# Turning the attended heads by 32x32 block transposes on VectorE instead of transposes on PE, with VectorE's order in an iteration laid out anew

## The reference, cut to what matters

```
x = x + tanh(g_ffn[0])   * L0_ffn(layernorm(x))
x = x + tanh(g_xattn[1]) * L1_xattn(layernorm(x), ctx, ctx, mask)
x = x + tanh(g_ffn[1])   * L1_ffn(layernorm(x))

# L1_xattn: 16 heads of 16 channels, 256 queries, 256 keys
scores = q_h @ k_h.T / 4                       # per head
attn   = softmax(scores)                       # over the keys
out_h  = attn @ v_h                            # 256 x 16 per head
out    = concat(out_h) @ w_o.T + b_o
```

## Time and profile before

| | us |
|---|---|
| median of 3 runs | 1606.79 |
| lowest and highest of the 3 | 1606.21, 1613.41 |
| the profiled execution | 1611.25 |
| its span, first to last instruction | 1609.4 |

### The profile page before, as it was taken

How to read it: one execution, slowest core, us unless ns; L and a number is a source line. 1 busy time by engine, 2 the same in 40 slices (tenths; PEclk the granted TensorE clock), 3 DMA queues, 4 the chain that set the end, 5 groups by cost and what they waited for, 6 DMA issues and landing times.

```text
span 1609.4 us, 42630 instructions
## 1 busy us (share of the span) xinstructions
PE 1483.6 (92%) x14155; PEld 1141.0 (71%) x14155; DVE 1318.3 (82%) x3187; ACT 1135.4 (71%) x2057; POOL 1030.6 (64%) x1392
## 2 busy tenths in 40 slices
PE   3899999999999974478999999999999999999997
PEld 2788888888888863245676677777777777767666
DVE  4798888888888876787888889898988888898732
ACT  7798888888888743265666666676666666666664
POOL 4688888888888743324456565666656565665445
PEclk8899999999999995588999999999999999999999
DMA  6322322322322002422222232233322332233100
GB/s 225 107 73 67 96 67 65 97 65 74 89 65 72 1 1 85 139 83 72 78 81 75 83 88 79 79 87 85 87 81 78 84 86 78 82 83 86 56 17 21
DMA packets 197690, 125.45 MB, mean 78 GB/s; under 512 B 44400, under 2 KB 196848, under 8 KB 197360
## 3 DMA queue, kind: packets, MB, share of 16 engines
q1 hardware_dynamic: 197616, 124.48, 26.7%
HBM read 92.69 MB, written 25.17 MB: 73 GB/s over the span
## 4 chain that ended last, share of the span: by engine, by line
PE 46%; SPq 6%; DMA 3%; DVE 2%; issue 2%; POOL 1%; ACT 1%; POOLq 0%
PE b_bank L1837 27%; PE b_bank L1912 6%; PE b_scoreT L1894 4%; PE b_score L1877 4%; PE b_bank L1845 2%; SPq L1293 2%; DMA b_nmT<-b_nm 1%; SPq L1282 1%; PE b_bank L1989 1%; SPq L1309 1%; PE b_bank L1927 1%; DMA b_yT<-b_y 1%; SPq L1318 1%; DVE b_nm L1653 1%; SPq L1326 1%
## 5 line engine op out<-in xcount | busy, mean ns | idle before, releaser
L1471 ACT ACTIVATE b_E<-b_scoreT 128x1024 f32<-128x1024 f32 x256 | 262.2, 1024 | 151.4 <-PE b_scoreT L1894 151.1
L1653 DVE TENSOR_REDUCE b_nm<-b_score 128x4 bf16<-128x1024 f32 x256 | 313.3, 1224 | 57.4 <-PE b_score L1877 51.2
L31 ACT ACT_TABLE_LOAD x157 | 201.4, 1283 | 18.6 <-PEq L1059 15.2
L1837 PE MATMUL b_bank<-f,b_YT 128*128 128x256 bf16 x1536 | 193.0, 277 | 4.7 <-POOL b_YT L1404 4.6
L890 PE MATMUL bank<-hT,W1T 128*128 128x256 bf16 x1536 | 183.3, 273 | 2.4 <-DVE hT L706 1.6
L1837 PE MATMUL b_bank<-b_hT,f 128*128 128x256 bf16 x1536 | 183.4, 273 | 0.8 <-DVE X L1749 0.8
L890 PE MATMUL bank<-W2T,G 128*128 128x256 bf16 x1024 | 171.0, 272 | 6.7 <-DVE GT L780 6.2
L1837 PEld LDWEIGHTS b_bank<-f,b_YT 128*128 128x128 bf16 x1536 | 144.7, 99 | 40.8 <-issue 19.3
L1837 PEld LDWEIGHTS b_bank<-b_hT,f 128*128 128x128 bf16 x1536 | 147.7, 98 | 30.4 <-issue 12.6
L890 PEld LDWEIGHTS bank<-hT,W1T 128*128 128x128 bf16 x1536 | 147.9, 98 | 27.8 <-ACT G L549 4.1
L1388 POOL TENSOR_TENSOR b_v<-b_v,b_e 128x512 f32<-128x512 f32 x32 | 40.7, 1270 | 194.1 <-DVE b_e L1734 194.1
(11 more groups left out here) (222 smaller groups left out, 3537.1 us busy)
## 6 DMA issues: line engine op xcount, KB each, us to landing
b_Q<-q_dram SPq DMA_DIRECT2D x192, 64.0 KB, 2.5
b_K<-k_dram SPq DMA_DIRECT2D x192, 64.0 KB, 2.7
xin<-in_x SPq DMA_DIRECT2D x32, 256.0 KB, 3.1
ctxn<-in_ctx SPq DMA_DIRECT2D x32, 256.0 KB, 2.8
mask_in<-in_mask SPq DMA_DIRECT2D x32, 256.0 KB, 3.0
X<-in_x SPq DMA_DIRECT2D x32, 256.0 KB, 4.0
ctxt<-in_ctxT SPq DMA_DIRECT2D x32, 256.0 KB, 4.2
b_ctxt<-in_ctxT SPq DMA_DIRECT2D x32, 256.0 KB, 2.8
```

Of the source, the lines that this page charges most:

```text
L31: act.add_instruction(mybir.InstLoadActFuncSet(name=nc.get_next_instruction_name(), act_func_set_id=which, ins=[], outs=[]))
L1471: nc.scalar.activation(E[:, pair:pair + 2], scoreT_ps[:, :, :, :], ACT.Exp).then_inc(sig["E"], 1)
L1653: nc.vector.tensor_reduce(pair, score_ps[:, :, :, :], AX.X, ALU.max, negate=True).then_inc(sig["nm"], 1)
L1837: last = nc.tensor.matmul(out_tile, lhs(i, k), rhs(j, k), start=start and k == chunks[0] and (i, j) == TERMS[0], stop=stop and k == chunks ...
```

## The change

VectorE turns the heads itself. heads_turned(c) is a transpose of each 32x32 block, straight from the PSUM bank to at; since one head's 32 rows fill one block of partitions, this puts tokens on partitions, 32 at a time. inverse_sums and attended divide in SBUF, and heads_back turns the blocks again into oF, channels down the partitions. ScalarE's heads_copy and PE's three groups of four transposes are gone. attended_high now reads oF, and attended_low moves from VectorE to GpSimd, behind rounded. The new steps for c = 0 all stand in the iteration of the values (stage a); those for c = 1 follow in the next one, but for heads_turned(1). Banks 8 and 9 lose the turns OT0, ON and OT1; AV01 and AV23 are now freed by heads_turned ("at").

VectorE's list is in another order. scaled, binades, mlp_columns, magic and base all stand between maxima 0 and 1; statistics_3 moves behind maxima 5 and heads_turned(0), statistics_2 behind maxima 6; mlp_normalised moves from the start of the next iteration to behind maxima 7. On GpSimd inverse_std_2 now stands ahead of silu_parts 0. PE's list is the same but for the transposes. On the host the rows of w_o and b_v are permuted to fit. Of the diff, in this order: GpSimd's new step and its list, ScalarE's attended_high, VectorE's new steps, PE's list.

```diff
+                def attended_low():
+                    pool.wait_ge(sig["onhi"], done(o))
+                    fence()
+                    nc.gpsimd.tensor_tensor(oT[:, 1], oF[:, :, :], oT[:, 0], ALU.subtract).then_inc(sig["onlo"], 1)
...
                 if o:
+                    attended_low()
                     inverse_std_3()
-                if h:
-                    silu_parts(h, 0)
                 if f:
                     inverse_std_2()
                 if h:
+                    silu_parts(h, 0)
                     silu_parts(h, 1)
...
                 def attended_high():
-                    act.wait_ge(sig["onT_mm"], done(o))
+                    act.wait_ge(sig["oF"], done(o, per=C))
...
+                def heads_turned(c):
+
+                    dve.wait_ge(sig["av_mm"], done(a, per=NH // HG, part=2 * c + 2))
+                    nc.vector.transpose(at[:, 2 * c:2 * c + 2].rearrange("p g b r -> p (g b r)"),
+                                        flat_bank(BANK[("AV01", "AV23")[c]])).then_inc(sig["at"], 1)
+
+                def inverse_sums(c, b):
+                    dve.wait_ge(sig["at"], done(b, per=C, part=c + 1))
+                    nc.vector.reciprocal(rsum[:, 2 * c:2 * c + 2, :], at[:, 2 * c:2 * c + 2, :, DK]).then_inc(sig["rsum"], 1)
+
+                def attended(c, b):
+                    dve.wait_ge(sig["rsum"], done(b, per=C, part=c + 1))
+                    nc.vector.tensor_tensor(on[:, c].rearrange("p b g d -> p g b d"), at[:, 2 * c:2 * c + 2, :, 0:DK],
+                                            rsum[:, 2 * c:2 * c + 2, :].rearrange("p g (b u) -> p g b u", u=1).to_broadcast(
+                                                [P, 2, Q32, DK]), ALU.mult).then_inc(sig["on"], 1)
+
+                def heads_back(c, b):
+
+                    dve.wait_ge(sig["on"], done(b, per=C, part=c + 1))
+                    if (due := done(b, back=1)) is not None:
+                        dve.wait_ge(sig["onlo"], due)
+                    nc.vector.transpose(oF[:, c, :], on[:, c].rearrange("p b g d -> p (b g d)")).then_inc(sig["oF"], 1)
...
-                if o:
-                    heads_transposed(0)
                 if m:
                     scores(0)
-                if o:
-                    heads_transposed(1)
...
-                if o:
-                    attended_transposed()
```

More of the change, by code:

```diff
@@ L1501, in attended_high @@
                 def attended_high():
-                    act.wait_ge(sig["onT_mm"], done(o))
+                    act.wait_ge(sig["oF"], done(o, per=C))
                     if (due := done(o, back=1)) is not None:
                         act.wait_ge(sig["proj_mm"], due)
[L1505 to L1512, removed]
+                    nc.scalar.activation(oT[:, 0], oF[:, :, :], ACT.Copy).then_inc(sig["onhi"], 1)
                 def values_copy():
@@ L1556, in iteration @@
                     exponential(6)
-                    heads_copy(0)
                     exponential(7)
@@ L1629, in mlp_normalised @@
                 def mlp_normalised():
[L1630 to L1631 removed]
+                    dve.wait_ge(sig["rs3"], done(o))
+                    if (due := done(o, back=1)) is not None:
                         dve.wait_ge(sig["hT_mm"], due)
                     for t in range(T):
[L1634 removed]
+                        last = nc.vector.tensor_scalar(hn[:, t, :], Xb(o, t), mv3[:, t, 0:1], rh3[:, t:t + 1], ALU.subtract,
                                                        ALU.mult)
@@ L1693, in keys_low @@
                     last.then_inc(sig["klo"], 1)
[L1695 to L1705, removed]
@@ L1775, in iteration @@
                     last.then_inc(sig["f1lo"], 1)
-                if o:
-                    attended(1)
+                if n:
+                    scaled()
+                    binades()
+                if h:
+                    mlp_columns()
+                if n:
+                    magic()
+                if h:
+                    base()
                 if m:
@@ L1785, in iteration @@
                     queries_low()
-                if o:
-                    attended_low()
                 if m:
                     maxima(3)
-                if h:
-                    mlp_columns()
-                if n:
-                    binades()
                 if at_iteration(half, parity, 1):
@@ L1797, in iteration @@
                     quantised_update()
-                if h:
-                    base()
-                if n:
-                    magic()
                 if m:
@@ L1809, in iteration @@
                     maxima(5)
+                if a:
+                    heads_turned(0)
+                if o:
+                    statistics_3()
+                if m:
                     maxima(6)
+                if f:
+                    statistics_2()
                 if w:
                     result()
-                if f:
-                    statistics_2()
+                if m:
+                    maxima(7)
+                if o:
+                    mlp_normalised()
+                if a:
+                    inverse_sums(0, a)
+                if f:
+                    attention_normalised()
+                if a:
+                    attended(0, a)
+                    heads_turned(1)
+                    heads_back(0, a)
                 if q:
                     mask_bias()
-                if m:
-                    maxima(7)
-                if f:
-                    attention_normalised()
                 if at_iteration(half, parity, 3):
@@ L2100, in col, with by_heads @@
         return np.ascontiguousarray(np.reshape(inputs[name], (-1, P)).T)
+    def by_heads(rows):
+        grid = np.reshape(rows, (2, 2, 4, DK, -1))
+        return np.ascontiguousarray(np.reshape(np.transpose(grid, (0, 2, 1, 3, 4)), (NH * DK, -1)))
     arrays = {
```

47 lines of the change are left out of this document (15 added, 32 removed).

## The result

The changed kernel takes 1859.9 us in the median of 4 runs (1858.3 to 1863.6), against 1607.0 for the kernel before beside it (4 runs, 1606.2 to 1613.4): a ratio of 1.157, 95% interval 1.153 to 1.160. It is slower by 252.9 us. The prediction had 1817 in a range of 1640 to 1890. Of the runs of the kernel before, one of those beside e9_store_between was slow, 1939.8 us at a granted clock of 0.74, and stands in no comparison here.

A forecast was written before the change was run, and what follows sets the result against it. PE was taken to set the pace at 28.2 us an iteration. 11.3 + 21.82 + 2.6 = 35.7 us, plus 0.85 for the clock, times 25 gave 915 against 704.6 us: +210, so 1817 us, range 1640 to 1890.

The forecast's parts named there:

- PE's 1.26 us: Three groups of four transposes leave PE at 0.42 us each: 1.26 us an iteration, at most 31 us in all.
- The 21.82 us: PE's time from scores(2) to the next scores(0), with two removed transpose groups of 0.42 us taken off.
- The transposes: VectorE's new 32x32 transposes: 0.68 us for 512 elements from PSUM, 0.42 us for 256.
- Maxima 0 to 1: VectorE's steps there are held up by GpSimd; maxima(1) ends at 11.25 us, scores(2) start at 11.3, 6.6 late.
- One for one: Between maxima 0 and 1, eight VectorE instructions go at GpSimd's pace, each waiting out the GpSimd instruction then running.
- The means named as a sign: If right, mean times of v, e, X and tg on VectorE rise to 0.7 us and more.
- Maxima 7 to the end: hidden(3) on PE waits for heads_turned(1), with hn and xh held by GpSimd: 2.6 us late.
- The clock: PE's idling lowers its granted clock; half the 1.7 us price of one drop taken, 0.85 us an iteration.
- one such drop is no rule: Reason given for charging only half of the single clock drop seen in the kernel before: 0.85 us.
- Rival 2: The clock pays in full, twice an iteration, for both PE idle stretches: +273 us, 1880 us; chance 0.12.
- (1): VectorE's forms aren't hindered at the new place: 29.8 us an iteration, 1648 us; chance 0.12, a part of it 0.16.
- (3): GpSimd becomes the bound: the projection waits 1.6 us for attended_low; +9 us, 1616 us; chance 0.04.

The follow-up runs named there:

- e9_store_between: e6_both with hn's transposes ahead of xh's, scaled between maxima 3 and 4, and SyncE's store ahead of row_of_maxima: 1602.09 us, ratio 0.9961 to the kernel before.
- e6_both: Changed kernel, five VectorE steps at old places, attended_low ahead of rounded, heads_turned(1) directly behind maxima 7: 1610.18 us, ratio 1.0013 to the kernel before.
- e5_pe_filled: Changed kernel with the query product made four times into the same bank, 36 matmuls more an iteration: 1827.84 us.
- experiments 1: Kernel before, PE's transposes kept, with scaled, binades, mlp_columns, magic and base put between maxima 0 and 1: 1816.99 us.
- e4_pool_narrow: Changed kernel with GpSimd's context_parts, both biases and silu_parts cut to 8 columns of each tile (output not the reference's): 1675.98 us.
- Experiment 3: Changed kernel with heads_turned(1) put directly behind maxima 7, ahead of mlp_normalised: 1777.64 us.
- e2_steps_back: Changed kernel with the five moved VectorE steps back at their old places and attended_low ahead of rounded on GpSimd: 1683.04 us.
- e8_low_last: e2_steps_back, but with attended_low left behind rounded on GpSimd, as the change has it: 1866.17 us.

## Why the prediction was right, and where its sizes were off

**What bounds the kernel.** Right: PE paces the kernel before, and the places between the maxima decide, not the totals. One reading was off, and nothing hangs on it: in the iteration that was read, two gaps of 0.21 are put down to another engine and not one (the second at 1223.89, to ScalarE's b_E).

**PE's 1.26 us.** Right in kind and small: taken off PE, they show up only in e6_both to e9_store_between, in part, as means of 27.7 to 27.9 us an iteration against 28.2. The 21.82 us from scores(2) to the next scores(0), which have 0.84 of them taken off, are borne out: e5_pe_filled needs 24.31 less the 2.46 of hidden(3), or 21.85.

**The transposes.** 0.68 and 0.42 were taken; 0.70 to 0.72 and 0.40 to 0.45 were measured. The Trainium skill (VectorE: DVE Perf Modes, "The three transpose paths") led to an estimate of 1.24 for the larger one, from its bfloat16 figure; the measurement decides, and it is 0.70.

**Maxima 0 to 1.** The mechanism was right and is shown by experiments 1 and 4. Ends behind scores(0), forecast and measured: scaled 4.2 and 4.4, binades 5.6 and 5.8, tg 6.1 and 6.3, up 7.3 and 6.5, magic 8.1 and 7.9, base 10.0 and 9.3, maxima(1) 11.25 and 10.5. "One for one" failed in the middle: up slipped into the gap where tg had just come through, and magic began just ahead of GpSimd's biases, which took 1.70 instead of 1.41; whether magic or base held them isn't shown. Two steps that the prediction ran unhindered were held: on (0.82 for 0.42) and dn (1.12 for 0.15), both with two inputs in SBUF. That the end comes out only 0.77 us too late, 19 us in all, is luck: the errors nearly cancel. The means named as a sign rose to 0.7 and more for X (0.77) and binades (1.34), but v and tg are at 0.58 and magic at 0.41.

The Trainium skill (SBUF — State Buffer, "Who interferes with whom") says that VectorE's two-port forms contend with GpSimd, its forms with two SBUF inputs with a GpSimd instruction that reads SBUF, and that the one that issues first blocks the other. The rows on on, dn and the biases agree, the last in GpSimd's disfavour.

**Maxima 7 to the end.** 2.6 us late was forecast and 2.46 measured, for the reason given: hn 1.92 and xh 1.48 stand ahead of the transpose, at GpSimd's pace. Experiment 3 shows that this order is the cause, and experiment 4 GpSimd's part in it: with GpSimd short, 0.46 of the 2.46 are left.

**The clock.** This is the term that was mis-sized. Half the price of one drop, 0.85 us an iteration, was taken; 27.02 - 21.82 - 2.46 = 2.74 us was measured, and experiment 5 gives 2.7 by another way. That is 1.89 us an iteration more than was taken, 47 us over 25 iterations. The step that failed is "one such drop is no rule": it was one, with a drop in every iteration. Rival 2 had the size better (3.4 us an iteration) but the wrong form: it priced two drops of 3.4 us, each at a loss of 1.7, one for each wait. In the changed kernel there is a single one of 6.8 us, which begins late in the longer wait, and none behind the wait at hidden(3). The Trainium skill (TensorE: Matmul & The Clock Gate, "What's actually happening") has the throttled state as the default that activity releases; that the drop comes back in all 25 iterations, and mostly goes (171 us to 31) when e5_pe_filled gives PE more to do, agrees. That the wait of 2.67 us at hidden(3) is followed by no drop here, by one in 15 of 25 iterations in e2_steps_back and by one in every iteration in e8_low_last, is not explained by any run.

**The sum.** 915 us were forecast for 25 iterations and 938.6 measured: +47 for the clock, -19 for the maxima, -4 at hidden(3), which makes 24. The other 18 us are filling and draining, which the prediction left out; together these are nearly the 43 us between 1817 and 1860. Rival 2's 1880 lies nearer to 1860 than the forecast does, but by luck: over the 25 iterations it was 39 us too long (978), the forecast 24 too short, and the 18 that both left out bring it nearer.

**The rivals.** (1) fell: VectorE's steps are held here, and with GpSimd short, in e4_pool_narrow, an iteration is near the 29.8 of this rival (30.2 and 31.7). (3) didn't happen here: attended_low ends 14.5 us behind scores(0), 2 later than forecast, but the projection is itself late, at 19.5. Its mechanism is real and dear, as e8_low_last shows with magic at its late place. The 1.6 us, worked out for the early one, wasn't tried. (4) fell: even with both delays removed, the gain is 0.4%.

**Not foreseen.** PE's wait of 0.80 us at xh's transposes, for a bank that ScalarE still reads: one group of transposes that used to fill this time is gone. It costs nothing while VectorE is later anyway, and shows up once that is mended (e6_both).

## What to carry to other kernels

Before steps of VectorE are moved, look at what GpSimd runs at the new place: the same instructions went from 0.42 to 1.34 us and from 0.15 to 1.12, and the wait went straight to PE. Where PE's idle time grows from tenths of a microsecond to several, put the clock into the sum at the full price of a drop for each iteration (here the wait of 5.5 us brought half clock in every iteration, one of 2.7 to 2.9 in none, some or all of them, by the kernel); and take the buffer that another engine waits for first, ahead of the work that nobody waits for. Work taken off the engine that sets the pace by 1.26 us an iteration gave under 0.5 at best here, where the engine that received it was busy 88% already.

## What the runs showed of the hardware that was not expected

- More work made the kernel faster: 36 matmuls more an iteration took PE's wait from 5.53 to 1.54 us, the half clock from 171 to 31 us of the steady part, and the time from 1860 to 1828.
- A VectorE instruction of two elements a partition with two inputs in SBUF (dn) can take 1.12 us beside GpSimd and takes 0.15 without. It ended 0.02 us behind the end of GpSimd's instruction: that end, not its own size, set how long it took.
- The 32x32 block transpose of 128x512 float32 values from PSUM takes 0.70 us, as long as an elementwise step of that size (xT, 0.68).
